# Two-layer decoder on one core: probabilities divided before the turn, values product transposed, in the three 16-wide-head attentions

## The reference

```python
x = x + gqa(ln(x))   # sign weights, 32 heads of 16, 8 key/value heads
x = x + xat(ln(x))   # cross attention, 32 heads of 128, masked
x = x + ffn(ln(x))   # block-sparse feed-forward
x = x + mqa(ln(x))   # 32 heads of 16, one key/value head, causal with position bias
x = x + cga(ln(x))   # cross attention to a context, 32 heads of 16, masked
x = x + moe(ln(x))   # linear with experts of rank 16

# the three that the change touches (gqa, mqa, cga), per sequence and head
scores = q @ k.T / 4
probs  = softmax(scores + bias_or_mask)      # max, subtract, exp, sum, divide
out    = probs @ v                           # 64 x 64 by 64 x 16
y      = concat_heads(out) @ Wo
```

## Time and profile before

| | |
|---|---|
| median of three runs | 2485.18 us |
| the profiled execution: its time, its span | 2487.27 us, 2485.5 us |
| mean granted TensorE clock | 0.978 |
| busy: TensorE, VectorE, ScalarE, GpSimd | 94%, 54%, 41%, 26% |
| gqa: first scores to last y product | 27.5 to 251 us |
| mqa: the same | 1827.6 to 2081 us |
| cga: the same | 2105.9 to 2355 us |

### The profile page before, as it was taken

How to read it: one execution, slowest core, us unless ns; L and a number is a source line. 1 busy time by engine, 2 the same in 40 slices (tenths; PEclk the granted TensorE clock), 3 DMA queues, 4 the chain that set the end, 5 groups by cost and what they waited for, 6 DMA issues and landing times. The chain is left out here.

```text
span 2485.5 us, 43032 instructions
## 1 busy us (share of the span) xinstructions
PE 2333.7 (94%) x17714; PEld 1861.3 (75%) x17714; DVE 1345.6 (54%) x2496; ACT 1028.3 (41%) x1749; POOL 651.5 (26%) x434
## 2 busy tenths in 40 slices
PE   7997999999999999999999799999989998999797
PEld 5776778777787877777787587787867766777586
DVE  5776534343333534334334786786756656665565
ACT  5654443445454453545444311101145444654331
POOL 1011231323324132322413341121132233432210
PEclk9999999999999999999999899999989998999988
DMA  4000111110111011110000300000010002100001
GB/s 150 2 18 2 52 44 42 35 52 21 55 45 52 35 35 52 35 52 18 35 35 18 114 25 0 0 0 0 0 60 1 2 1 77 35 2 1 8 22 68
DMA packets 22354, 80.82 MB, mean 33 GB/s; under 512 B 3360, under 2 KB 5536, under 8 KB 16032
## 3 DMA queue, kind: packets, MB, share of 16 engines
q1 hardware_dynamic: 22176, 78.28, 9.0%
HBM read 74.08 MB, written 4.19 MB: 31 GB/s over the span
## 5 line engine op out<-in xcount | busy, mean ns | idle before, releaser
L2349 PE MATMUL xat_TP<-xat_Wo,xat_oT_hi 128*128 128x512 f32 x1024 | 322.4, 396 | 5.8 <-issue 5.8
L103 PE MATMUL xat_G<-xat_xnT_hi,xat_Wq 128*128 128x512 f32 x768 | 249.3, 397 | 0.0
L2349 PEld LDWEIGHTS xat_TP<-xat_Wo,xat_oT_hi 128*128 128x128 f32 x1024 | 187.3, 188 | 58.2 <-issue 22.4
L2047 POOL TENSOR_TENSOR xat_T<-xat_T,xat_mask 128x512 f32<-128x512 f32 x64 | 81.8, 1303 | 525.9 <-DVE xat_T L2129 525.9
L2349 PE MATMUL xat_TP<-xat_Wo,xat_oT_lo 128*128 128x512 f32 x512 | 199.5, 390 | 0.0
L2156 DVE TENSOR_TENSOR X<-X,xat_TP 128x512 f32<-128x512 f32 x128 | 87.0, 680 | 202.3 <-PE xat_TP L2349 202.3
L2120 DVE RECIPROCAL xat_q_inv_rms<-xat_OT 128x16 f32<-128x16 f32 x32 | 8.3, 258 | 328.9 <-PE xat_OT L2276 328.9
L103 PEld LDWEIGHTS xat_G<-xat_xnT_hi,xat_Wq 128*128 128x128 f32 x768 | 144.3, 188 | 34.1
L103 PE MATMUL ffn_H<-ffn_w,ffn_xnT_hi 128*128 128x448 f32 x512 | 147.2, 368 | 10.2 <-DVE ffn_h_kept L1209 10.1
L1122 ACT ACTIVATE ffn_hT_hi<-ffn_TP 128x384 fp32r<-128x384 f32 x64 | 34.9, 545 | 293.9 <-PE ffn_Y L1258 252.0
L103 PE MATMUL xat_G<-xat_xnT_lo,xat_Wq 128*128 128x512 f32 x384 | 151.8, 395 | 0.0
(11 more groups left out here) (457 smaller groups left out, 5743.8 us busy)
## 6 DMA issues: line engine op xcount, KB each, us to landing
xat_weights_raw<-in_Cq_q SPq DMA_DIRECT2D x16, 1024.0 KB, 4.8
xat_weights_raw<-in_Cq_o SPq DMA_DIRECT2D x16, 1024.0 KB, 4.8
xat_kv_raw<-in_Cq_kv SPq DMA_DIRECT2D x7, 1024.0 KB, 6.9
cga_ctxT_raw<-in_ctxT SPq DMA_DIRECT2D x4, 1024.0 KB, 6.5
out<-X SPq DMA_DIRECT2D x4, 1024.0 KB, 4.3
ffn_weights_raw<-in_w1T SPq DMA_DIRECT2D x8, 448.0 KB, 4.0
ffn_weights_raw<-in_w SPq DMA_DIRECT2D x7, 512.0 KB, 4.4
X<-in_x SPq DMA_DIRECT2D x2, 1024.0 KB, 6.9
```

The source lines that it names most:

```text
L103: last = eng.matmul(out, a, b, start=(n == 0), stop=(n == len(steps) - 1))
L2047: eng.tensor_tensor(T[:, n, :, :], T[:, n, :, :], mask[:, :].unsqueeze(1).to_broadcast([P, ROWS, SEQ]), ALU.add)\
L2349: last = eng.matmul(TP[m % 2][:, :], x, w, start=(n == 0), stop=(n == len(steps) - 1))
```

## The change

- After the exponential VectorE sums the rows of both halves (one instruction, 1024 wide) and inverts the sums (`invert(s-1)` in step s), and GpSimd multiplies the exponentials by the inverse, in place (`normalize(u)`, two a step). `turn(u)` waits for this product instead of the exponential. Its place in TensorE's queue is the same.
- VectorE's order in step s: gqa maxima, subtractions, `invert(s-1)`; mqa and cga additions, `invert(s-1)`, maxima. GpSimd's order in mqa and cga: both divisions of pair s-1, then both subtractions of pair s.
- The column of ones goes. `values(s)` is called once a step, for both halves: stationary is `Vbd` (128 x 32, two heads), moving the turned probabilities (2 x 64 columns); the result is the transposed output, four pairs of heads in four groups of 32 partitions of the bank O. PT has 4 buffers instead of 2.
- `normalize` on VectorE, `o_normed` and the items ot0 to ot3 go. High and low part are taken from O once a tile (`keep_o` on ScalarE, `low_o` on VectorE, in even steps).
- gqa: the last addition to x (`add_y`) and the product of the layer norm (`normed`) go from VectorE to GpSimd, and the low parts for the next block take their place in GpSimd's steps.

```diff
@@ vector queue @@
-            def normalize(s):
-                t = s // 2
-                src = O[:, 0:2 * CH * W1].rearrange("p (h d) -> p h d", d=W1)
-                eng.wait_ge(pv_done.sem, pv_done.at(0, 2 * s + 2))
-                n = chain(eng.reciprocal(ri[:, s % 2, :], src[:, :, HD]))
...
-                eng.tensor_tensor(dst, src[:, :, 0:HD], ri[:, s % 2, :].unsqueeze(2).to_broadcast([P, 2 * CH, HD]),
-                                  ALU.mult).then_inc(on_ready.sem, 1)
+            def invert(s):
+                at = 2 * s % RING
+                eng.wait_ge(exp_ready.sem, exp_ready.at(0, 2 * s + 2))
+                eng.reduce_sum(rs[:, s % 2, :], T[:, at:at + 2, :, :].rearrange("p u h s -> p (u h) s"), AX_X)\
+                   .then_inc(summed.sem, 1)
+                eng.wait_ge(summed.sem, summed.at(0, s + 1))
+                if s >= 2:
+                    eng.wait_ge(norm_ready.sem, norm_ready.at(0, 2 * s - 2))
+                eng.reciprocal(ri[:, s % 2, :, :].rearrange("p u h -> p (u h)"), rs[:, s % 2, :])\
+                   .then_inc(inv_ready.sem, 1)
...
-                if 3 <= s < LASTP + 3:
-                    normalize(s - 3)
-                if s < LASTP:
-                    if sign:
-                        shift_pair(s)
-                    else:
-                        find_max(2 * s)
-                        find_max(2 * s + 1)
+                if s < LASTP and sign:
+                    shift_pair(s)
+                if 1 <= s < LASTP + 1:
+                    invert(s - 1)
+                if s < LASTP and not sign:
+                    find_max(2 * s)
+                    find_max(2 * s + 1)
+                if 4 <= s < LASTP + 4 and s % 2 == 0:
+                    low_o((s - 4) // 2)
@@ gpsimd queue @@
+            def normalize(u):
+                s, r = divmod(u, 2)
+                eng.wait_ge(inv_ready.sem, inv_ready.at(0, s + 1))
+                row = T[:, u % RING, :, :]
+                eng.tensor_tensor(row, row, ri[:, s % 2, r, :].unsqueeze(2).to_broadcast([P, CH, SEQ]), ALU.mult)\
+                   .then_inc(norm_ready.sem, 1)
...
-                for s in range(LASTP):
-                    shift(2 * s)
-                    shift(2 * s + 1)
+                for s in range(LASTP + 1):
+                    if s > 0:
+                        normalize(2 * s - 2)
+                        normalize(2 * s - 1)
+                    if s < LASTP:
+                        shift(2 * s)
+                        shift(2 * s + 1)
@@ scalar queue @@
+            def keep_o(n):
+                i, t = divmod(n, ST)
+                eng.wait_ge(pv_done.sem, pv_done.at(0, 2 * n + 2))
+                if n >= 2:
+                    eng.wait_ge(y_done.sem, y_done.at(0, n - 1))
+                eng.activation(oh[:, t % 2, :, :], O[:, :].rearrange("p (c n) -> p c n", c=KC), ACT.Copy,
+                               scale=scp[:, KC + 1:KC + 2] if sign else 1.0).then_inc(oh_ready.sem, 1)
@@ tensor queue @@
             def turn(u):
-                eng.wait_ge(exp_ready.sem, exp_ready.at(0, u + 1))
+                eng.wait_ge(norm_ready.sem, norm_ready.at(0, u + 1))
...
-            def values(u):
+            def values(s):
...
+                for b in range(2):
+                    for r in range(2):
+                        for g in range(2):
+                            pair = 2 * r + g
+                            out = O[pair * 2 * HD:(pair + 1) * 2 * HD, :].rearrange("p (c n) -> p c n", c=KC)
+                            last = eng.matmul(out[:, 2 * half:2 * half + 2, b * SEQ:(b + 1) * SEQ],
+                                              Vbd[:, i % 2, 2 * t + b, pair, :],
+                                              PT[:, (2 * s + r) % PTS, :, g, b * SEQ:(b + 1) * SEQ],
+                                              start=True, stop=True, tile_position=(0, pair * 2 * HD))
...
                 if s < LASTP:
                     scores(s)
                 if 3 <= s < LASTP + 3:
-                    values(2 * s - 5)
+                    values(s - 3)
                 for item in filled(s, 0):
                     make(item)
                 if 2 <= s < LASTP + 2:
                     turn(2 * s - 3)
-                    values(2 * s - 4)
@@ attention_plan @@
         if i > 0:
-            b[0], b[1] = [(i - 1, "ot2")], [(i - 1, "y2")]
-            b[2], b[3] = [(i - 1, "ot3")], [(i - 1, "y3")]
+            b[1], b[3] = [(i - 1, "y2")], [(i - 1, "y3")]
         if i < NST:
             for t in range(2):
-                b[2 * t + 4].append((i, f"ot{t}"))
                 b[2 * t + 5].append((i, f"y{t}"))
```

More of the change, by code:

```diff
@@ L304, in small_attention @@
         pre = mem.sig("prologue_vector", PRE, 1)
-        pre_pool = mem.sig("prologue_pool", 9 if sign else 3, 1)
+        pre_pool = mem.sig("prologue_pool", 7 if sign else 1, 1)
         k_done, kbd_ready = mem.sig("k_product", 1), mem.sig("kbd_ready", 1)
@@ L366, in freed @@
                 return q_ready, q_ready.at(i, c + 1)
-            if name[0] == "o":
-                return ol_ready, ol_ready.at(i, c + 1)
-            return y_added, y_added.at(i, (c + 1) * (2 if sign else 1))
+            return y_added, y_added.at(i, 2 * c + 1 if sign else c + 1)
         def filled(s, part):
@@ L457, in keep @@
                     if i == 0:
-                        eng.wait_ge(pre_pool.sem, pre_pool.at(0, 3))
+                        eng.wait_ge(pre_pool.sem, pre_pool.at(0, 1))
                     for e in range(2):
                         rows = slice(e * SEQ, (e + 1) * SEQ)
-                        last = eng.activation(Vbd[rows, i % 2, :, :, e * W1:e * W1 + HD],
+                        last = eng.activation(Vbd[rows, i % 2, :, :, e * HD:(e + 1) * HD],
                                               bank[rows, :].rearrange("p (b j d) -> p b j d", b=SB, j=4), ACT.Copy)
                     last.then_inc(v_ready.sem, 1)
[L464 to L468, removed]
             def exponent(u):
@@ L628, in _ @@
             count = [0]
-            links = [0]
             def step(ins):
@@ L783, in _ @@
                     for t in norm_slots(i).get(s, ()):
-                        ln.vector_xn(eng, i, t)
+                        if sign and t == 0:
+                            ln.vector_inverse(eng, i)
+                        elif not sign:
+                            ln.vector_xn(eng, i, t)
             for item in filled(LASTP + 3, 1):
                 take(item)
-            assert count[0] == PRE and links[0] == vec.per * NST, (count, links)
+            assert count[0] == PRE, count
         @block.tensor
@@ L846, in make @@
                     last.then_inc(v_done.sem, 1)
-                elif name[0:2] == "ot":
-                    t = int(name[2])
-                    eng.wait_ge(on_ready.sem, on_ready.at(i, 2 * t + 2))
-                    for c in range(KC):
-                        last = eng.transpose(bank[:, c * P:(c + 1) * P], On[:, t % 2, c * P:(c + 1) * P], ident[:, :])
-                    last.then_inc(ot_done.sem, 1)
                 else:
```

121 lines of the change are left out of this document (60 added, 61 removed).

## The result

The changed kernel takes 2528.0 us (median of four runs, 2525.2 to 2531.5), the kernel before 2484.6 beside it: ratio 1.0175, 95% interval 1.0158 to 1.0193, 43 us slower. The forecast was 2496, in a range from 2479 to 2514. The profiled execution has a span of 2529.6 us, 44.1 above the one before, at a mean granted clock of 0.956 (0.978 before).

The account below looks back on a forecast made before the run. TensorE's queue looked like the bound before; afterwards loops through VectorE and GpSimd would set gqa's steps and some of mqa's and cga's. Stage sums of -2.5 us plus 13.5 for the clock gave +11 on 2485.2: 2496, range 2479 to 2514.

Parts of the forecast that it names:

- the loop: gqa: scores, VectorE's inversion, GpSimd's division, turn and next scores form a chain that sets every step at 6.72 us.
- The value form: TensorE's value products: 16 instructions in four column groups take 0.53 us, saving 0.65 us per step.
- that rival: Column groups do not overlap with two-part moving data, 1.2 us more in some 20 steps of mqa and cga: 2540, chance 0.03.
- The step that failed: mqa and cga: TensorE's own work per step of a pass, 3.54 to 8.4 us, mostly keeping the bound.
- The clock: Idle TensorE drops to half clock in 21 gaps over three stages, 0.65 us each: +13.5 us, bounds 0 to 36.
- GpSimd's second loop: mqa and cga: sum, two divisions, two subtractions, exponential and hops through GpSimd take 6.35 us a step, binding the last pass.
- y2's stall: Step 1 of a pass: y2 waits longer for x2's low part behind the inversion; 10.1 us in mqa, 8.3 in gqa.
- That the clock would hold: Rival: the loops bind but the granted clock stays at 1.00, leaving only -2.5 us: 2483, chance 0.2.
- That TensorE stays the bound in mqa and cga and the whole gets faster: Rival: x2's low part comes within 3 us of the scores, giving back 22 us: 2474, chance 0.1.
- That GpSimd and VectorE get in each other's way: Rival: each division and subtraction on GpSimd takes 0.25 us more, +17 us: 2513, chance 0.17.

Follow-up runs that it names:

- The filler: Each group of value products issued four times in the last pass of the three stages, against the changed kernel: 2516.7 us, ratio 1.0117.

## Why the prediction was wrong

**The direction and the loop.** Slower was forecast as likeliest, for the reason that held: the division stands between exponential and turn, the turn ahead of the next scores. Putting the inversion ahead of what waits for scores takes 43 us off, in gqa alone; putting the scores ahead of the turn takes 51, a covered seam included. Its length was forecast as 6.72 us and is 6.82: the hand-over to GpSimd is 1.57 for 1.54, TensorE takes up its result in 0.06 for 0.03, and a turn that starts out of idle time hands over in 0.59, not 0.53. Over some 30 steps that is 3 us.

**The value form** (0.53 for 16 in four column groups, from the earlier trace rows) is 0.57 to the next product (201.03 to 201.60 in gqa's timeline). Column groups overlap with two-part moving data; that rival is out.

**The step that failed** is "TensorE's steps of a pass are 3.54, 6.4, 5.5, 8.4, 6.6, 8.4, 5.5, 8.4". They were made from the old steps by taking off what was removed, a value group and an output turn. These instructions were also what lay between two turns that share one bank, so taking them off uncovered ScalarE's copy: 6.44, 7.57 and 6.48 us in the even steps. That is 0.9 to 1.0 us in three steps of each middle pass and two of the first, eight a stage; in mqa and cga together some 15 us of the 32 by which 2496 missed. In gqa the loop is longer than those steps anyway. The prediction asked of every edit costed at nothing what work hides it, and did not ask of the removed work what it had been hiding. The two kernels without a division show this term by itself, 27.4 us over twelve passes.

**The clock** was the right mechanism and the second term that failed, by its size. It was put at 0.65 for each of 21 pieces at the lower level, 3.4 us long, 13.5 us. In steps 0 to 31 of the three stages together the changed kernel's profile is at the lower level for 105 us, where before was for 10: 95 us more are 28 such pieces, not 21. The filler's profile is at it for 51 us, 54 less, and its kernel is 11.3 us shorter (16.3 by the profiled executions), so a piece of 3.4 us costs 0.7 to 1.0. At that price 28 pieces are 20 to 28 us, 6 to 14 more than forecast. This is an estimate: it gives the whole of the filler's gain to the clock and takes one price everywhere. What one piece costs depends on what it falls on: in mqa's step 17 above, where it falls on y2's products, it is 1.6 us. In gqa's third pass step 17 is 9.05 us in the changed kernel and 8.16 in the filler's profile, but step 19 is 6.82 and 7.95, with the same instructions in both.

**GpSimd's second loop** was forecast as 6.35 us in mqa's last pass. At the full clock (cga's last pass in the filler's profile, 44.9 us) it is 5.62 and 7.45 in turn, 6.54 on average: with 43.6 forecast for steps 24 to 31, 1.3 us more a stage, 2.5 in both.

**y2's stall** in step 1 of a pass was forecast as 10.1 us in mqa and cga and 8.3 in gqa. Measured are 9.8 in mqa and cga and 8.16 in gqa where the clock held, and up to 11.5 and 9.05 where it did not. Right.

Together 15 (the seams) + 3 (gqa's loop) + 6 to 14 (the clock) + 2.5 make 27 to 34 us, and 32 were missed. The seams and the loops are read from steps; the clock's share is the estimate above, so how much is left over stays open.

**The rivals.** That the clock would hold is refuted by the windows. That TensorE stays the bound in mqa and cga and the whole gets faster is refuted, though a reordered queue gives just that. That GpSimd and VectorE get in each other's way is refuted: of the changed kernel's 320 multiplies and subtractions on GpSimd 304 take 1.03 to 1.06 us, as the earlier trace rows had for the subtractions, and the 16 others, up to 1.24, add 3 us of its own time at most. The Trainium skill (GPSIMD Engine Reference, Key points) has GpSimd elementwise at about half of VectorE's speed. Here it is 1.02 us an instruction beside VectorE's 0.61 to 0.68, a ratio of 1.5 to 1.7; the measurement decides, and the row was the better price.

## What to carry to other kernels

Before work is put between two instructions of an in-order queue, write down what stands behind the waiting one and close the loop: here 43 us were lost or won by which of two calls stood first, on either of two engines. Of work that is removed, ask what it had been covering: two users of one buffer that it kept apart are now neighbours. And in this case a loop that left TensorE idle was longer than the sum of its links at full clock, 7.28 and 7.72 for 6.82 us.

## What the runs showed that was not expected

- TensorE work added to idle time made a kernel faster: with 285 more instructions in gqa's last pass the granted clock there was 0.97 and not 0.85, and with three such stretches the kernel took 11.3 us less. In a kernel whose last pass of mqa ran at 0.91 the same filling cost 6.3 us.
- At the clock's lower level a turn takes 1.12 us against 0.60 to 0.66. It comes right behind the gap, so what gets longer is the very link that the loop waits for, and the idle time does not absorb it.
- What an edit is worth depends on what stands elsewhere: maxima and subtractions first gained nothing with the turn ahead of the scores (2532.5 against 2528.0 us) and gave 47 us with the turn behind them.
